# A 7x7 convolution with the column-parity identity applied twice, and the split of its input into fp16 parts moved between engines

## What is computed

```python
x = x + conv3x3(sign(_gn(x)), round(tanh(w0))) * alpha        # layer 0
x = x + irfft2(einsum('bchw,cohw->bohw', rfft2(_gn(x))[:56], w1))   # layer 1
x = x + conv7x7(_gn(x), w2) + bias                            # layer 2, written with an FFT, equal to a 7x7 convolution, padding 3
x = x + window_attention(_gn(x), ...)                         # layer 3: focused linear attention in 8x8 windows
```

## Time and profile before

| | |
|---|---|
| median of 3 runs | 12865.6 us (12861.85 to 12867.78) |
| profiled execution, its own time | 12852.61 us |
| its span (first to last instruction) | 12850.9 us |
| mean granted TensorE clock | 0.94 |
| busy: TensorE, its weight loads, DVE, ACT, POOL | 90%, 81%, 60%, 39%, 19% |

### The profile page before, as it was taken

One profiled execution on the slowest core, in us unless ns is written; L12 is line 12 of the kernel. 1 busy time (PEld: TensorE's weight loads), 2 busy tenths in 40 slices (PEclk: granted clock), 3 DMA queues, 4 the chain that ended last, 5 costly groups with the idle time before them and its releaser, 6 DMA issues.

```text
span 12850.9 us, 310865 instructions
## 1 busy us (share of the span) xinstructions
PE 11510.5 (90%) x134269; PEld 10468.0 (81%) x134269; DVE 7650.6 (60%) x14071; ACT 5006.4 (39%) x6088; POOL 2397.7 (19%) x1544
## 2 busy tenths in 40 slices
PE   6888878866999999999999999999999999999995
PEld 4666668866888888888888888888888888888884
DVE  6666632223666666666666666666666666666665
ACT  4555531111434444444343434344343434343433
POOL 0000000001222222222222222222222222222221
PEclk9999988878999999999999999999999999999997
DMA  7888879971111111111111111111111111111100
GB/s 182 215 212 216 212 184 242 246 185 44 33 42 35 33 34 34 34 33 34 33 34 33 34 33 34 33 38 45 38 33 33 34 33 34 33 34 33 34 22 15
DMA packets 969176, 947.89 MB, mean 74 GB/s; under 512 B 588704, under 2 KB 933776, under 8 KB 948176
## 3 DMA queue, kind: packets, MB, share of 16 engines
q1 hardware_dynamic: 944400, 708.58, 25.1%
q0 software_dynamic: 23488, 220.21, 4.8%
...
## 4 chain that ended last, share of the span: by engine, by line
PE 39%; DVE 22%; ACT 7%; issue 6%; DMA 2%; POOL 0%; DVEq 0%; SPq 0%; ACTq 0%; POOLq 0%
PE c_ps L875 28%; DVE c_qk L1258 3%; PE c_ps L970 3%; DVE c_s L1279 3%; DVE c_s L1274 3%; ACT c_sq L1095 3%; ACT c_sq L1101 3%; DVE c_v L1250 2%; DVE c_qk L1246 2%; PE c_ps L983 2%; PE c_ps L1001 2%; DVE c_cube L1273 2%; DVE c_xr L1186 2%; PE c_ps L938 1%; PE c_ps L991 1%
## 5 line engine op out<-in xcount | busy, mean ns | idle before, releaser
L875 PE MATMUL c_ps<-c_xp,c_wst 128*128 128x228 f16 (+1 forms) x59136 | 6168.5, 263 | 201.6 <-DVE c_cv L1226 126.4
L875 PEld LDWEIGHTS c_ps<-c_xp,c_wst 128*128 128x128 f16 x59136 | 5705.0, 98 | 567.2 <-issue 313.9
L1111 ACT ACTIVATE c_att<-c_ps 128x896 f32<-128x896 f32 x224 | 205.5, 917 | 2551.1 <-PE c_ps L991 2551.1
L1406 POOL TENSOR_TENSOR c_xr<-c_kvm,c_xr 128x896 f32<-128x896 f32 x224 | 468.4, 2091 | 3484.4 <-ACT c_kvm L1118 3484.4
L1391 POOL TENSOR_TENSOR c_xr<-c_cv,c_xr 128x448 f32<-128x448 f32 x448 | 591.5, 1320 | 2016.8 <-ACT c_cv L1086 2016.8
L528 PE MATMUL b_ps<-b_xs,b_wt 64*64 64x64 f32 x6384 | 778.2, 298 | 171.9 <-DVE b_xj L504 163.4
L528 PEld LDWEIGHTS b_ps<-b_xs,b_wt 64*64 64x64 f32 x6384 | 690.2, 219 | 175.1 <-issue 175.0
L528 PE MATMUL b_ps<-b_xj,b_wt 64*64 64x64 f32 x6384 | 779.2, 297 | 12.6 <-issue 12.5
L938 PE MATMUL c_ps<-c_wqkv,c_xn 64*128 64x192 f32 x6272 | 664.1, 354 | 120.2 <-DVE c_xr L1186 45.0
L1401 POOL TENSOR_TENSOR c_cube<-c_sq,c_qk 128x896 f32<-128x896 f32 x224 | 661.3, 2952 | 583.0 <-ACT c_sq L1095 583.0
L1118 ACT ACTIVATE c_kvm<-c_ps,c_pbias 64x448 f32<-64x448 f32 x896 | 564.0, 629 | 452.4 <-PE c_ps L1001 444.0
(11 more groups left out here) (156 smaller groups left out, 16315.1 us busy)
## 6 DMA issues: line engine op xcount, KB each, us to landing
...
out<-c_xr SPq DMA_DIRECT2D x448, 224.0 KB, 3.1
...
```

What stands on the lines that cost most here:

```text
L875: ins = pe.matmul(ps[:, which // 2, col:col + ROWS * width], wst[:, ws, pr, first + k].rearrange("p q o -> p (q o)"), xp[:, xs, kind, ROWS ...
```

## The change

1. **The convolution.** The parity identity is applied twice: four column phases, nine products (`PRODUCTS`) with 17 taps for four output columns. A chunk is now 8 row pairs (`CROWS`), one per attention step: 17 x 4 x 3 = 204 matmuls of 8 x 28 = 224 columns, 7 chunks per image.
2. **Planes.** Nine planes (sums and differences of phases) instead of three. POOL makes three operations for each row chunk, DVE two more (`differ`), 4 x 29 x 3 elements each.
3. **High part.** ACT makes it (`high_part`), 9 x 4 x 30 = 1080 elements; DVE makes only the low part.
4. **Ring.** The fp16 planes are a ring of 24 row pairs instead of a whole image; each turn copies three rows twice. A high part waits for the chunks that still read its place.
5. **PSUM.** Products go in pairs through four banks (0, 1, 6, 7). The inverse DFT uses a ring of four banks instead of five; attention uses banks 2 to 5; TensorE now waits for the copy of transposed q before kv.
6. **Output.** ACT takes the three shared products (`take_b`: b1 of two products, b2 of one) with scale and bias, DVE the other six (`take_t`, t3 to t8; t3 and t6 to a buffer, the others added straight into every fourth column of x), POOL adds the shared ones in four operations of 448 elements (`add_conv`).
7. **Start.** A convolution chunk c waits for row chunks up to 2c + 2, so the first waits for three.
8. New tables of pieces; `att` shares the space of `qt`.

The core of the diff:

```diff
-SUMS = ((4, 3, 0, 1, W // 2 + 1), (0, 4, 1, 0, W // 2), (7, 4, 2, 0, W // 2))
+PRODUCTS = (("o", 0, 2), ("o", 2, 2), ("o", 1, 2), ("a", 1, 2), ("a", 0, 2), ("a", 2, 2), ("c", 1, 2), ("c", 0, 2),
+            ("c", 2, 1))
+CONV_BANKS = (0, 1, 6, 7)
...
-QBANK = (2, 6, 4, 2)
+QBANK = (2, 4, 2, 4)
+FIRST_QBANK = (4, 2, 4, 2)
-PIECES = (24, 75, 145, 165, 215, 235)
-FIRST_PIECES = (0, 100, 190, 215, 270, 290)
-SECOND_PIECES = (50, 90, 150, 170, 220, 240)
+PIECES = (12, 30, 62, 114, 130, 168, 184)
+FIRST_PIECES = (0, 0, 77, 147, 166, 198, 204)
+SECOND_PIECES = (12, 39, 70, 116, 131, 170, 186)
...
+                    if i == 0:
+                        if p == 0:
+                            pe.wait_ge(s.lo_done, n * NCH + min(2 * c + 3, NCH))
@@ TensorE, attend
-                    project(l, range(4))
+                    project(l, a, range(2))
                     conv(pieces[0])
+                    project(l, a, range(2, 4))
+                    conv(pieces[1])
...
+                pe.wait_ge(s.qt_taken, l + 1)
                 pe.wait_ge(s.scaled, l + 1)
@@ ACT, bring
                 for k in range(EARLY):
                     padded_chunk(n, odd, k)
+                    if k:
+                        high_part(n, k - 1)
+                high_part(n, EARLY - 1)
@@ ACT, attend
                 pad()
...
                 act.activation(sq[:], qk[:], ACT.Square).then_inc(s.u2_done, 1)
                 if a < A7 - 1:
                     window_rows(l + 1, a + 1, odd)
+                high(0)
+                conv(True)
...
                 act.activation(sq[:], cube[:].rearrange("p q k r c -> p r q k c"), ACT.Square).then_inc(s.u6_done, 1)
...
                                ).then_inc(s.qt_taken, 1)
+                conv(False)
+                high(1)
@@ DVE, bring
                 for k in range(EARLY):
-                    low_part(n, k)
+                    differ(n, k)
+                    if k:
+                        low_part(n, k - 1)
+                low_part(n, EARLY - 1)
@@ DVE
+            def take_t(n, odd, c, p):
+                chunk = n * A7 + c
+                kind, f, _ = PRODUCTS[p]
+                dve.wait_ge(s.prod_done, NP * chunk + min(2 * (p // 2) + 2, NP))
@@ DVE, attend
+                conv_before(7)
+                conv_before(8)
                 if a:
                     take_qkv(l, a)
+                pad("differ", 0)
...
+                stats()
...
+                conv(3)
+                pad("low", 0)
+                pad("differ", 1)
...
+                conv(4)
                 dve.wait_ge(s.num_done, l + 1)
...
+                conv(5)
+                conv(6)
+                pad("low", 1)
```

422 lines of the change are left out of this document (235 added, 187 removed).

## The result

The changed kernel takes 13101.2 us (median of 4 runs, 13098.7 to 13121.3), beside 12863.7 us for the kernel before on the same chip (12856.3 to 12867.8): ratio 1.0189, 95% interval 1.0171 to 1.0206. It is slower, the side to which the forecast leaned with a chance of 0.48, and inside the wide band of 12400 to 13300 us; but the forecast said 0.3% and it is 1.9%, above the range of its own case (12780 to 13030). The sum missed by 196 us.

A forecast was written before the change was run, and what follows sets the result against it. TensorE ends last, a few us ahead of the attention chain, which would take back nearly all the gain. 12852.6 + 65 - 44 + 17 + 9 = 12900, plus half of 13: 12905 us, range 12780 to 13030.

The forecast's parts named there:

- its own case: The forecast's main case: nearly all the matmul gain is given back, 12905 us, chance 0.37.
- The walk: Steady attention step followed instruction by instruction from P, the issue of the projection: 36.8 us against 36.44 before.
- the four waits: TensorE in the steady step: 1.9 us for the q cube, 1.6 scaled keys, 1.1 kvm, 2.0 attention sum.
- the wait of t4 for matmul 144: On DVE between num and the inverse: t4 waits for products 4 and 5, adding 2.0 us to the chain.
- Rival A: TensorE still ends last, the added work falling in DVE's and ACT's idle time: 11860 us, chance 0.08.
- rival D: The clock falls inside steps after TensorE's waits, one 3 us restart a step: 13463 us, chance 0.06.
- the evacuation: Step 1: output evacuation by ACT holds the second batch back some 1.8 us; 38.6 against 39.2, gain 0.6.
- the start of an image: From the norm, the convolution waits for three row chunks, so TensorE idles 10.9 us longer; 50.2 against 46.4.
- ACT normalise 2 x 0.79: At an image's start, ACT's normalisation of each row chunk: two operations of 0.79 us in a round of 5.55 to 5.6.
- B: Rival: half of the insertions miss the steady step's chain, 2 us a step less, 12533 us; chance 0.24.
- C: Rival: GpSimd comes late with more operations, 1.5 us a step onto the chain, 13184 us; chance 0.22.
- E: Rival: convolution matmuls with runs of 28 columns instead of 56 are slower, 13200 us; chance 0.03.

The follow-up runs named there:

- Experiment 1: Changed kernel with VectorE's t sum 4 moved behind the addition of the local attention: 12722.0 us.
- Experiment 3: Changed kernel with VectorE's key-value mask moved ahead of t sum 3, the first low part and the second differences: 13075.8 us.
- Experiments 1 to 3: Experiment 1, Experiment 3 and a run between them: changed kernel with ScalarE's first high part and b sums behind the second Square, 13020.8 us.
- Experiment 4: Changed kernel with ScalarE's normalisation reading contiguous columns instead of every fourth; its output is not the layer's: 13025.0 us.
- Experiment 10: Changed kernel with VectorE's low part of the chunk before ahead of this chunk's differences, at the start of an image only: 13097.5 us.
- experiment 12: Fastest kernel until then (12470.7 us), with the first part of each image's first attention step moved into the image's start and its matmuls dealt anew: 12341.7 us.
- experiment 6: Changed kernel with GpSimd's query cube ahead of its differences for the second chunk of planes: 13250.5 us.

## Why the prediction was right, and where it was too small

**The steady step: right in its mechanism.** The walk named the four waits, the place of the second Square, and the wait of t4 for matmul 144, and put the step at 36.8 us. Where the granted clock is 1.00 and the ring does not turn it is 36.3 (step 2) and 36.1 (step 3); the walk was 0.5 to 0.7 too long there, with one of its four waits, 1.6 us for the scaled keys, absent and the one for the query cube about 0.9 longer. Experiment 1 prices its largest term directly: 2.0 to 2.3 us a step for t4, walk 2.0. Rival A is refuted by the same run, for it would have made the move worthless. The four banks of the inverse transforms cost nothing, as taken (+0.1 us an image). Its price list was good too: low part 1.27 (taken 1.3), high part 1.10 (1.1), b1 0.63 (0.65), additions with a step of four columns 1.38, between the 1.14 of the unstrided row and the 1.7 that the forecast had estimated by the Trainium skill. The Trainium skill, GPSIMD Engine Reference, section on performance pitfalls, gives half as much again for such reads; this trace shows a fifth more, with the step in one of the two inputs and in the output.

**The first term that was missing: the clock was put into a rival and kept out of the sum.** The walk took all TensorE durations at full clock. It had itself four waits of 1.1 to 2.0 us in the step, and rival D priced a restart at 3 us, chance 0.06. In the trace the price is smaller, about 1 us in steps 2 and 3 and 2 in step 1, and it comes in part of the steps: on average 1.1 us in step 1 (40.55 against 39.5 at full clock), 1.1 in step 2, 0.9 in step 3, together some 3 us an image. It is D at a third to two thirds of its price, and it came on top of the forecast, not instead of it.

**The second: the turn of the ring was listed as part of the change and given no price.** It costs step 4 1.45 us (above). Step 1 has it too: at a granted clock of 1.00 it takes 39.5 us, which is step 2's 36.3 and the 1.8 of the evacuation that the walk had, and 1.4 more. That makes an estimated 2.9 us an image, as much as the clock. Experiment 3, which takes the low part out of the way, makes step 4 as short as step 3 at equal clock. Steps 2 to 6 together gained nothing (183.1 against 183.0) where 1.3 was expected.

**Part of the nearness is luck.** The clock, the ring and the start of an image (2.6 us, below) come to some 8.5 us an image; the miss is 6.4, since the walk was too long by half a us or more in most steps. With chances of 0.41 for faster and 0.48 for slower, that the time came out on the slower side says little for the forecast; the places of the waits in the step say more.

**Step 1: +1.8 instead of -0.6.** The walk had the evacuation's wait. It had neither the ring (the high part takes 1.87 us in the step below) nor what follows in 16 of the 30 images, whose step 1 takes 41.4 to 41.8 us. TensorE's timeline at the start of a step 1 that lasted 41.4 us:

```profile
7322.19 0.92 PE L976 MATMUL c_ps<-c_wqkv,c_xn 64*128 64x192 f32 x8
7324.93 1.39 PE L976 MATMUL c_ps<-c_wqkv,c_xn 64*128 64x192 f32 x8 [1.81 <-ACT c_kvm L1178]
7326.25 2.42 PE L913 MATMUL c_ps<-c_xp,c_wst 128*128 128x224 f16 x12
7328.60 1.25 PE L976 MATMUL c_ps<-c_wqkv,c_xn 64*128 64x192 f32 x12
```

After the wait of 1.81 us for the output's evacuation the next twelve matmuls take 2.42 us, so that the second half of the projection is issued 6.4 us after P; in the steady step it is 2.83. The clamp starts 9.1 us after P (7331.29), where the walk had 7.35 (5.55, and 1.8 for the evacuation). In the other 14 images step 1 takes 39.5 us. In 7 of these its granted clock is 1.00; in the other 7 there is as long a spell at half clock as in the slow ones, but it begins 16 us after P and not 3, and it costs nothing. So the same spell costs 2 us where it meets the projection, and none where TensorE has time to spare. The kernel before has such spells in its step 1 too (39.2 us in 21 images, 37.6 at 1.00 in 9): the 39.2 with which the walk compared its 38.6 had one, and the 38.6 had none. Experiments 1 to 3 each shorten step 1 by 1.7 to 2.1 us.

**The start of an image: +13.3 instead of +10.9.** The failed term is "ACT normalise 2 x 0.79". The 0.79 was of a row without stride, while the new instruction reads every fourth column; it takes 1.20. A chunk round is 6.1 us, not 5.55. Experiment 4 gives the 0.4 back and with it 2.1 of the 2.4 us. But the start had a second thing wrong with it that the result could not show: the walk took the start of the convolution for what the first step waits for. Experiment 10 moves that start by 2.1 us for nothing, experiment 12 moves the attention's front and gains 4.3 us an image, 1.2 of them in step 1. So the +13.3 and the -6.9 are no two independent terms: the first step's end is set by ScalarE's order, and the start of the convolution is inside it. The walk added an idle TensorE to a step of 36.8 us and came to 50.2 from norm to P1; in the image above, counted as in the walk from VectorE's last norm instruction, it is 52.2 (7270.00 to 7322.20).

**B, C and E.** B, that half of the insertions miss the chain, did not come. C, GpSimd late by 1.5 us a step, came only as far as TensorE: the query cube ended 13.7 to 13.9 us after P where the walk had 12.7, but the second Square of step 2, at 14.23, was not late (walk 14.35). Bringing the cube forward (experiment 6) made things worse, because it met VectorE's; a kernel in which GpSimd is early without that was not run. E, slower matmuls, did not come either: in the first image 1428 of them take 143.36 us, 0.100 each, against 0.099 before.
